# Attention and a gated feed-forward layer on one core: the shift rows' transfers move from SyncE's queue to ScalarE's

## What is computed

```
x = x + layernorm(attention(layernorm(x)))      # 32 heads of 16 channels, rotary positions, causal
x = x + layernorm(ffn(layernorm(x)))            # silu(x Wg) * (x Wu), 1408 wide, then Wd

attention: q, k, v = x Wq, x Wk, x Wv (+ biases)
           weights = softmax(mask(q k^T / 4));  out = (weights v) Wo
```

## Time and profile before

| | us |
|---|---|
| median of three runs | 3098.64 |
| the profiled execution's own time | 3105.56 |
| span of the profiled execution | 3103.8 |

### The profile page before, as it was taken

How to read it: one execution, slowest core, us unless ns; L and a number is a source line. 1 busy time by engine, 2 the same in 40 slices (tenths; PEclk the granted TensorE clock), 3 DMA queues, 4 the chain that set the end, 5 groups by cost and what they waited for, 6 DMA issues and landing times. The chain is left out here.

```text
span 3103.8 us, 59189 instructions
## 1 busy us (share of the span) xinstructions
PE 2601.8 (84%) x19584; PEld 1260.9 (41%) x19584; DVE 2199.6 (71%) x6495; ACT 1330.8 (43%) x1710; POOL 1020.0 (33%) x1051
## 2 busy tenths in 40 slices
PE   3788878788778888888887888853999999999997
PEld 1343434444334344444344444321444444444443
DVE  4878879788778797887788877836555545545544
ACT  2455555555545555555455555524222222222222
POOL 3454455454544554545446545310000000000000
PEclk9899999999999899998999989976999999999999
DMA  3222332322322323223223232222111111111111
GB/s 138 84 78 86 86 89 65 110 89 65 106 92 80 94 63 108 90 63 112 90 75 98 64 100 76 73 88 87 41 54 41 68 42 53 68 41 54 68 41 41
DMA packets 94356, 237.07 MB, mean 76 GB/s; under 512 B 13456, under 2 KB 63888, under 8 KB 80912
## 3 DMA queue, kind: packets, MB, share of 16 engines
q1 hardware_dynamic: 94096, 233.64, 23.7%
HBM read 148.39 MB, written 84.15 MB: 75 GB/s over the span
## 5 line engine op out<-in xcount | busy, mean ns | idle before, releaser
L673 DVE CUSTOM_DVE_ANT_0 mx<-mx,causal 128x512 f32<-128x512 f32 (+3 forms) x2048 | 944.2, 517 | 267.6 <-PE mx L798 265.4
L525 ACT ACTIVATE probs<-ts,exp_scale 128x1024 f32<-128x1024 f32 x640 | 712.7, 1114 | 723.3 <-PE ts L812 723.2
L451 POOL TENSOR_SCALAR_AFFINE_SELECT probs<-probs 128x512 f32<-128x512 f32 x512 | 321.0, 644 | 774.7 <-ACT probs L525 774.7
L1218 DVE SCALAR_TENSOR_TENSOR hidden<-gu,up_scale,silu 128x512 f32<-128x512 f32 x176 | 131.9, 750 | 417.4 <-PE gu L1268 407.7
L798 PE MATMUL mx<-kT,qT 64*128 64x512 f16 (+3 forms) x2048 | 263.3, 315 | 181.3 <-DMA kT<-slots 89.6
L1077 ACT ACTIVATE silu<-gu,gate_scale 128x512 f32<-128x512 f32 x176 | 120.9, 687 | 631.1 <-PE gu L1268 631.1
L1052 POOL TENSOR_TENSOR f_rstd<-f_var,f_neg_half 128x4 f32<-128x4 f32 x32 | 32.3, 1009 | 928.5 <-DVE f_var L1195 647.5
L812 PE MATMUL ts<-qT,kT 64*128 64x512 f16 (+3 forms) x2048 | 258.1, 310 | 71.0 <-DMA qT<-shift_rows 57.6
L826 PE MATMUL xb<-probs,vs 128*32 128x512 f32 (+3 forms) x4096 | 312.1, 446 | 1.0 <-POOL probs L451 1.0
L1266 PE MATMUL gu<-f_xT_hi,gate_hi 128*128 128x512 f16 x704 | 267.7, 380 | 52.2 <-issue 52.2
L673 DVE DVE_READ_ACCUMULATOR2_ANT row_max<- 128x1 f32 x2048 | 283.6, 138 | 0.0
(11 more groups left out here) (145 smaller groups left out, 4597.8 us busy)
## 6 DMA issues: line engine op xcount, KB each, us to landing
slots<-half_hi SPq DMA_DIRECT2D x512, 64.0 KB
qT<-slots SPq DMA_DIRECT2D x128, 256.0 KB, 3.9
kT<-slots SPq DMA_DIRECT2D x128, 256.0 KB, 3.9
xn<-x SPq DMA_DIRECT2D x16, 1024.0 KB, 4.9
xr<-x SPq DMA_DIRECT2D x16, 1024.0 KB, 5.6
slots<-half_lo SPq DMA_DIRECT2D x256, 64.0 KB
x<-xr SPq DMA_DIRECT2D x16, 1024.0 KB, 5.6
f_xn<-x SPq DMA_DIRECT2D x16, 1024.0 KB, 4.7
```

The lines of the kernel that those rows point to most:

```text
L451: nc.gpsimd.affine_select(out=d, in_=d, compare_op=ALU.is_ge, fill=0.0, base=0, pattern=[[0, HG], [1, P]], channel_multiplier=-1).then_inc ...
L525: nc.scalar.activation(probs[:, g % 2, u, :, :], ts[:, :, :], ACT.Exp, scale=exp_scale[:, 0:1]).then_inc(ts_read, 1)
L673: last = nc.vector.tensor_tensor_reduce(out=scores, in0=scores, in1=causal[:, T - P * (qt + 1):T], scale=1.0, scalar=-3e38, op0=ALU.add, o ...
```

## The change

The four transfers of `place_shift`, with their two waits, leave SP's list (u = 2) and stand in ACT's list directly behind `read_shift` (u = 1). Nothing else changes: the same number of transfers, sizes, semaphores, buffers.

```diff
-            def place_shift(i, g):
-
-                turned_rows, placed = held(sp, NG * i + g + 1), held(sp, 64 * (NG * i + g))
-                sp.wait_ge(shift_read, turned_rows)
-                wait_if_any(sp, shift_in, placed)
-                for j in range(2):
-                    for pair in range(2):
-                        at = 4 * j + 2 * pair
-                        sp.dma_start(qT[SLOT * j + 3 * DH:SLOT * j + 3 * DH + 2, g // 2, 2 * (g % 2) + pair, :],
-                                     shift_rows[at:at + 2, g % 2, :]).then_inc(shift_in, 16)
...
-                    if u == 2 and exists(i + (g + 1) // NG):
-                        place_shift(i + (g + 1) // NG, (g + 1) % NG)
...
+            def place_shift(i, g):
+                act.wait_ge(shift_read, NG * i + g + 1)
+                wait_if_any(act, shift_in, 64 * (NG * i + g))
+                for j in range(2):
+                    for pair in range(2):
+                        at = 4 * j + 2 * pair
+                        act.dma_start(qT[SLOT * j + 3 * DH:SLOT * j + 3 * DH + 2, g // 2, 2 * (g % 2) + pair, :],
+                                      shift_rows[at:at + 2, g % 2, :]).then_inc(shift_in, 16)
...
                     if u == 1 and exists(i + (g + 1) // NG):
                         read_shift(i + (g + 1) // NG, (g + 1) % NG)
+                        place_shift(i + (g + 1) // NG, (g + 1) % NG)
```

## The result

The changed kernel takes 3130.64 us (median, 3124.9 to 3133.99) against 3099.94 us in the same comparison: ratio 1.0085, 95% interval 1.0066 to 1.0104. By the ratio that is 26 us slower; the two medians lie 31 us apart, since the kernel before scattered from 3097.47 to 3110.02 us. Its profiled execution has a span of 3128.9 us, 25.1 us more than the one shown ahead. The stall that the change aims at is gone, and more than its worth came back at three other waits.

The account below looks back on a forecast made before the run. PE and DVE were taken to bound the attention phase by turns, both stopping for keys at step 30. Losses of 43.5 us less gains of 40.4 gave about +3 on 3098.64, so 3102 us; range 3078 to 3150.

Parts of the forecast that it names:

- The gain at step 30: Step 30, sequences 1 to 14: PE's stall for late shift rows goes, 1.29 to 2.17 us each, 25.1 us together.
- The gain at step 5: Step 5, sequences 0, 1, 13, 14, 15: PE's stall for shift rows counts as far as DVE idles, 15.3 us.
- g = 1: Group 1's issues on ACT: 0.73 us late, DVE with about 1 us of work at step 9; about 1 us lost.
- B: On ACT, time from the copy's end to the next exponential with four issues between: 2.65 us.
- g = 0: Steps 1 to 4: oT 1.28 us late in the middle sequence, partly hidden by DVE's slack; 12.5 us lost in all.
- g = 5: Group 5's issues: 1.35 us late before the 6.72 us stop for keys, whose chain is untouched; nothing lost.
- g = 6 and 7: Steps 31 to 34 and 36 to 39: oT late by up to 0.73 and 1.35 us; losses 7.5 and 20.3 us.
- "about 1" of the signs: Sign to look for: PE's idle time before L844 grows from 0.17 to about 1 us at g = 0 and 7.
- g = 2, 3, 4: Groups 2, 3: gaps of 2.6 to 3.05 us hide the block; group 4: 1.35 late, DVE has work; nothing lost.
- The rival of the queues: ACT's and SP's issues hinder each other, lengthening the chain to the keys and ACT's block: 3112 to 3187 us, chance 0.25.
- The rival "swallowed": Delays on ACT are smaller or made up within the loop's end branch: 3060 to 3094 us, chance 0.20.
- The rival "the stalls stay": PE waits for the shift rows' landing, not their issue, so gains vanish: 3142 us, chance 0.07.

Follow-up runs that it names:

- spread kernel: Changed kernel with ACT's four issues split: one behind the copy, one ending u=2, two ending u=3; 3066.45 us, ratio 0.9881.
- under kernel: Changed kernel with ACT's issues split: one behind u=2's exponential, one ending u=2, two behind u=3's exponential; 3071.45 us, ratio 0.9883.

## Why the prediction came out as it did

The range held the time (3078 to 3150) and the likeliest sign was slower, but the number, 3102 us, was 29 us short. The number by itself, +3 us, foretold next to no change; that "slower" led with 0.46 came from the rivals. Against the sections:

- **The gain at step 30: right.** Forecast 25.1 us, measured 26.7.
- **The gain at step 5: right within 1 us.** For the sequences 1, 13 and 14 it was 2.8 + 2.1 + 4.3 = 9.2 us; their sections 4 to 13 fell by 8.6, partly by luck: 2.9 in 1, only 0.5 in 13 (a slow piece told of below ate the rest) and 5.3 in 14. The section's sum is only -3.7, since each of the other eleven lost 0.3 us at g = 1 (medians 25.98 to 26.30), and one of them 1.6 us more: 5 us where I had 1.
- **B: right where ACT issues alone.** Forecast 2.65 us, measured 2.60 at g = 4 and 2.65 at g = 6, with 2.38 to 2.43 us of issues (forecast 2.42). Elsewhere, beside SP's issues, the row grew: 2.61 at g = 0, 2.93 at g = 1 (B 2.82 and 3.15), 2.58 and 2.53 at g = 5 and 7 (B 2.80 and 2.75).
- **g = 6 and 7: right.** 7.5 and 20.3 us forecast in 15 sequences (18.9 of the 20.3 in the 14 of the table), +7.1 and +20.0 measured. That g = 7 was right in size is partly luck, for DVE's 2.27 us there was not in the working: steps 35 to 38 lost 23.5 us, and 38 to 40 gave 3.5 back. PE's wait for `oT` grew to 0.67 us and not to the "about 1" of the signs, since PE had by then stood 0.67 us for the exponential.
- **g = 2, 3, 4: right.** Steps 13 to 25 do not move by 0.1 us; at g = 2 and 3 ACT's 3.04 us of idle time hide the block, as foretold.
- **g = 0: the step that failed.** Forecast 12.5 us, measured 22.9. I followed the block to `oT` and PE and took off DVE's slack of 0.26 us. But `biased` stands between, and DVE's own list has the product of `biased` in the same step: DVE had waited 0.20 us for it there in the kernel before too (0.3 us at most, 26 times in the loop's stretch, nearly all at steps 2 and 37), so it had no slack against ACT at all. Of the queue "exponential, `biased`, `oT`" I priced the first and the last. `oT` has an idle time of its own that hides 0.62 us of the block; `biased` has none. Sequence 13 shows it best, with g = 0 alone on ACT (the first two lines are of the kernel before):

```profile
1699.29 1.11 ACT L525 ACTIVATE probs<-ts,exp_scale 128x1024 f32<-128x1024 f32 x1 [0.68 <-PE ts L812]
...
1701.02 0.69 DVE L650 TENSOR_TENSOR roped<-biased,cos_sb 128x512 f32<-128x512 f32 x1
...
1711.66 1.11 ACT L526 ACTIVATE probs<-ts,exp_scale 128x1024 f32<-128x1024 f32 x1 [2.80 <-DMA qT<-shift_rows]
...
1713.38 0.69 DVE L662 TENSOR_TENSOR roped<-biased,cos_sb 128x512 f32<-128x512 f32 x1 [2.24 <-ACT biased L513]
```

The exponential comes 2.12 us later behind the copy, and steps 0 to 4 take 12.10 us instead of 9.98: 2.12 more, the whole delay, at a granted clock of 1.00 at the head of both. The sum had 0.9 us a sequence. The rest of the 10.4 us is B, 2.82 instead of 2.65 (about 2 us, an estimate), and, in the changed kernel, the clock: in the sequences 13 and 14 it stood at 0.50 at the head where the kernel before had 1.00, in 11 the other way, about 2 us in all (an estimate too).
- **g = 5: the second.** I gave it nothing, and named a change of this chain as a sign of being wrong. ACT's results there are indeed free, but the chain to the keys grew by 0.5 to 0.6 us a sequence, +7.2 us. SP's rows at that place, which answer to the earlier trace rows:

```profile
917.03 1.29 SPq L349 DMA_DIRECT2D slots<-half_hi  x2
918.36 0.57 SPq L349 DMA_DIRECT2D slots<-half_lo  x1
918.97 1.33 SPq L349 DMA_DIRECT2D slots<-half_hi  x2
920.35 0.74 SPq L349 DMA_DIRECT2D slots<-half_lo  x1
```

ACT issues from 918.8 on. The second pair takes 1.33 us instead of 1.17 and the last send 0.74 instead of 0.57: of the four issues of the rival's sum the last two grow, by 0.14 to 0.17 us each and not by 0.56. The fetch behind them then starts 0.5 to 0.6 us later than before. The rival of the queues was thus real at about a quarter of its price. The Trainium skill (Perfetto Trace Analysis, "DMA Instruction — HWDGE (DVE, Sync)") has the generator of descriptors locked for one sequencer at a time with the wait inside the profiled duration. The rows agree in kind; that issues side by side grow by some 0.15 to 0.2 us speaks for an exclusive part that is small beside the 0.57 us (an estimate; no run parts it).

- **The rival "swallowed"**: nothing was made up within the branch: the 12 times that the loop turns back took 53.6 us before and 53.1 after. (The working had 13 times, and its 3078 took off the 24 us of the loop's end alone, though it also set B at 2.45, which was worth 8 more.) **The rival "the stalls stay"**: none did.

Sum: 10.4 us at g = 0, 7.2 in the chain and 4 at g = 1 make 21.6 us. The forecast for the 14 sequences of the table comes to about +5.6 (gains 25.1 and 9.2, losses 18.9, 7.5, 12.5 and 1), 21.3 below the sections' +26.9; the other differences cancel. Outside them sequence 0 added 3.4 us and sequence 15 with what follows gave 5.2 back, which makes the 25.1 us of the span.

## What to carry to other kernels

A transfer that an engine issues holds that engine's list for the whole issue (0.58 us here), unless one of its instructions is still running meanwhile. Put issues behind a long activation, and don't put several in one piece directly behind a wait for the engine's own last result. When an engine is to be held for some time, list every result queued behind it and look in the trace for each consumer's idle time just before it uses that result; a consumer that already idles 0.1 or 0.2 us has no slack, whichever engine it is. Four issues in three places (0.6, 0.6 and 1.2 us) left the kernel 37 us faster, the same four in one piece of 2.4 to 2.9 us left it 26 us slower.

## What the runs showed of the hardware that I had not expected

ACT's sequencer issues transfers at the same time as its data path runs an activation (215 of 298 us in the spread kernel); the profile before, in which SP alone issues, could not show it.

TensorE's granted clock falls to 0.50 (1.2 GHz) at places that differ from one sequence to the next. Around step 30, after PE's wait for the keys, it does so in nearly every sequence of every kernel. At the head of a sequence it does in 6 to 12 of the 14, by kernel. The heads of sequences 12 and 13 of the kernel before, after PE stood 3.97 and 3.57 us at the loop's branch (columns: stretch, length, busy us of PE, PEld, DVE, ACT, POOL, granted clock, DMA share, GB/s):

```profile
1571.54:1575.54 4.00, 4.00 (x14) 1.02 (x13) 2.90 (x7) 1.14 (x2) 0.00 (x0) 0.50 0.16 43
1694.96:1698.96 4.00, 4.00 (x28) 1.59 (x28) 4.00 (x11) 2.69 (x3) 0.63 (x1) 1.00 0.27 72
```

Steps 0 to 4 took 12.39 us in the one and 9.98 in the other. The kernels with all transfers on ACT have a further place. In sequences 9 and 13 of the changed kernel the section from 5 to 13 took 24.1 to 24.2 us instead of 22.5. The timeline of PE at step 11, sequence 9, and the same stretch of sequence 8:

```profile
1253.66 0.61 PE L781 MATMUL xb<-w_hi,aT_hi 128*128 128x512 f16 x1 [1.00 <-DVE xT_lo L636]
1254.06 0.63 PE L782 MATMUL xb<-w_lo,aT_hi 128*128 128x512 f16 x1
...
1127.40 0.39 PE L781 MATMUL xb<-w_hi,aT_hi 128*128 128x512 f16 x1 [1.00 <-DVE xT_lo L636]
1127.63 0.38 PE L782 MATMUL xb<-w_lo,aT_hi 128*128 128x512 f16 x1
```

Their windows:

```profile
1253.60:1257.00 3.40, 3.34 (x8) 1.16 (x9) 1.86 (x6) 0.37 (x1) 0.64 (x1) 0.50 0.22 63
...
1127.30:1130.00 2.70, 2.60 (x12) 1.08 (x12) 1.91 (x6) 0.41 (x1) 0.64 (x1) 1.00 0.30 82
```

After the same 1.00 us of idle time PE is granted 0.50 (1.2 GHz) in one sequence and 1.00 (2.4 GHz) in the other, for some 3.4 us, and the step ends 1.6 us later. It struck 2 of the 14 sequences in the changed kernel, 5 in the spread and 8 in the under kernel, none at this place in the kernel before, where it fell instead near step 5 in the three sequences with the longest stalls there (1, 13 and 14). The faster kernels thus pay up to 13 us for it. Whether it makes a part of the scatter between executions isn't shown, since one execution of each kernel was profiled. What decides between two such sequences no run here shows.
